# A two-layer graph kernel: the prologue in another order, inverse roots by GpSimd's power

## What is computed

```python
h = relu(layernorm(x))
w_norm = (weight - mean(weight)) / std(weight, ddof=1)
weight_q = quantise to 3 bits and a sign, range wgt_alpha
xq = quantise h to 4 bits, range act_alpha
support = relu(matmul(xq, weight_q))            # scaled by the deltas
support_q = quantise support to 4 bits, range act_alpha2
x1 = x + matmul(adj, support_q)                 # scaled back
out = x1 + attention_layer(relu(layernorm(x1)), adj, ...)
```

## Time and profile before

| | |
|---|---|
| three runs | 160.69, 160.95, 161.58 us; median 160.95 |
| profiled execution | 160.78 us, span 158.9 us |
| mean granted TensorE clock | 0.983 |
| busy, share of the span | TensorE 89%, VectorE 71%, ScalarE 69%, GpSimd 24% |
| DMA | 27.44 MB, mean 173 GB/s |

### The profile page before, as it was taken

The page is one execution under the profiler, slowest core; times in us unless marked ns, Lnnn a source line. Parts: engine busy times, 40 slices in busy tenths (PEclk is TensorE's granted clock), DMA queues, the critical chain, the costliest instruction groups (busy, mean ns, idle before and its releaser), DMA issues.

```text
span 158.9 us, 2206 instructions
## 1 busy us (share of the span) xinstructions
PE 141.7 (89%) x702; PEld 111.9 (70%) x702; DVE 112.1 (71%) x242; ACT 109.2 (69%) x157; POOL 37.4 (24%) x123
## 2 busy tenths in 40 slices
PE   0093999999999999999999999999999999999930
PEld 0093766667676667788888888888888888889920
DVE  0799799898936355997975667876779779624461
ACT  3637878889988587918937999999995966121000
POOL 2134251423320000006070111012016265221100
PEclk9999699999999999999999999999999999999997
DMA  2999999993221100052399899993101101110102
GB/s 47 373 412 416 398 394 426 414 323 55 51 59 40 37 0 0 0 171 97 45 341 400 250 379 359 342 388 144 66 0 66 66 4 66 66 66 0 68 8 68
DMA packets 11982, 27.44 MB, mean 173 GB/s; under 512 B 5184, under 2 KB 5440, under 8 KB 9920
## 3 DMA queue, kind: packets, MB, share of 16 engines
q1 hardware_dynamic: 11824, 27.27, 48.2%
q10 hardware_dynamic: 144, 0.00, 0.0%
HBM read 22.02 MB, written 4.19 MB: 165 GB/s over the span
## 4 chain that ended last, share of the span: by engine, by line
PE 87%; DVE 7%; DMA 3%; issue 1%; SPq 0%; DVEq 0%
PE acc L925 28%; PE acc L927 28%; PE acc L907 9%; PE acc L893 9%; PE acc L908 9%; DMA w_sb<-weight 3%; PE acc L935 2%; PE acc L879 1%; DVE w_st L747 1%; DVE st L679 1%; DVE h_i L704 1%; DVE w_i L750 1%; DVE w_q L756 1%; DVE ring L742 1%; PE acc L938 0%
## 5 line engine op out<-in xcount | busy, mean ns | idle before, releaser
L925 PE MATMUL acc<-sup,hi 128*128 128x512 f32 (+1 forms) x208 | 76.4, 374 | 0.1
L927 PE MATMUL acc<-sup,lo 128*128 128x512 f32 (+1 forms) x208 | 76.3, 373 | 0.0
L925 PEld LDWEIGHTS acc<-sup,hi 128*128 128x128 f32 x208 | 39.2, 188 | 7.3 <-issue 0.5
L927 PEld LDWEIGHTS acc<-sup,lo 128*128 128x128 f32 x208 | 39.2, 188 | 6.8
L370 ACT ACTIVATE junk<-raw,below 128x2048 uint8<-128x2048 f32 x16 | 31.8, 1989 | 0.0
L512 POOL TENSOR_SCALAR nm<-mv 128x1 f32<-128x1 f32 (+2 forms) x20 | 13.3, 665 | 65.8 <-DVE ve L689 65.8
L907 PE MATMUL acc<-sup,hi 128*128 128x512 f32 x64 | 27.9, 436 | 0.0
L720 DVE TENSOR_TENSOR lo<-raw,hi 128x2048 fp32r<-128x2048 f32 x11 | 25.1, 2285 | 2.9 <-ACT hi L359 2.9
L908 PE MATMUL acc<-sup,lo 128*128 128x512 f32 x64 | 25.1, 393 | 0.0
L727 DVE SCALAR_TENSOR_TENSOR ring<-ring,rs,x_sb 128x512 f32<-128x512 f32 x15 | 11.0, 750 | 14.8 <-POOL rs L521 12.2
L359 ACT ACTIVATE hi<-raw 128x2048 fp32r<-128x2048 f32 x11 | 21.0, 1910 | 0.3 <-PE acc L908 0.2
(11 more groups left out here) (78 smaller groups left out, 117.6 us busy)
## 6 DMA issues: line engine op xcount, KB each, us to landing
raw<-adj_t SPq DMA_DIRECT2D x16, 1024.0 KB, 7.0
out<-ring SPq DMA_DIRECT2D x15, 256.0 KB, 4.2
x_sb<-x SPq DMA_DIRECT2D x3, 1024.0 KB, 14.4
w_sb<-weight SPq DMA_DIRECT2D x4, 256.0 KB, 5.0
x_sb<-x SPq DMA_DIRECT2D x2, 256.0 KB, 5.0
x_sb<-x SPq DMA_DIRECT2D x1, 512.0 KB, 6.3
out<-ring SPq DMA_DIRECT2D x2, 128.0 KB, 2.2
h_iT<-h_i SPq DMA_TRANSPOSE x8, 2.4
```

The source lines that it names most:

```text
L925: nc.tensor.matmul(bank[:, cols], part(hi, k % PARTS, j), sup[:, j, cols], start=(j == 0), stop=False)
L927: ins = nc.tensor.matmul(bank[:, cols], part(lo, k % PARTS, j), sup[:, j, cols], start=False, stop=(j == T - 1))
```

## The change

- **Transfers.** The scalars have no transfer of their own; each row of the weight is followed by the four scalars (516 columns instead of 512), and VectorE reads them from block 0. x tile 0 is loaded from ScalarE's queue. SP starts with the weight.
- **Inverse roots.** Reciprocal, Sqrt and refining are replaced by one GpSimd `tensor_tensor` with `ALU.pow` and an exponent of -0.5, in both layers, for the weight and for tile 15. ScalarE's relu takes the quantising constant as its scale, and GpSimd multiplies the negated mean by it.
- **Statistics.** ScalarE sums tiles 0 and 1 (two passes each). VectorE takes two tiles per turn up to j = 5.
- **Order.** TensorE: transposes 0, 24 warm-ups, transposes 1, 6 warm-ups, support 0, support 1, aggregate 0, transposes 2 and 3, aggregate 1, support 2, then for each j support(j-1), transposes(j), aggregate(j-2). Around the sums stand 16 and 12 warm-ups. ScalarE and VectorE are ordered to match.

The diff's core (the renaming of semaphores and tiles is left out):

```diff
-    WARM_SUMS, WARM_FIRST, WARM_T, WARM_S = 14, 14, (12, 4), (0, 12)
+    WARM_SUMS, WARM_FIRST, WARM_T = 16, 12, (24, 6)
...
+        w_sb = sb("w_sb", [P, KD, D + 4], F32)
...
-            load_x(0)
             for k in range(KD):
                 load_w(k)
...
-            def root(n, a, m):
-                act.wait_ge(inverse_ready, n)
-                nc.scalar.activation(rs[:, a:a + m], rv[:, a:a + m], ACT.Sqrt).then_inc(root_ready, 1)
...
+            act.dma_start(x_sb[:, 0, :], x[0:P, :]).then_inc(x_in[0], 16)
+            sums(0)
             relu1(0)
+            sums(1)
             relu1(1)
+            copy_T(0)
             act.wait_ge(w_bias, 1)
             round_w(2)
+            round_w(3)
+            copy_T(1)
+            split_piece(0)
+            relu_sup(0)
+            relu_sup(1)
+            relu1(2)
+            split_piece(1)
+            relu1(3)
+            copy_T(2)
+            copy_T(3)
+            split_piece(2)
+            relu1(4)
+            relu1(5)
+            relu_sup(2)
+            split_piece(3)
+            for j in range(4, T + 2):
+                if j <= T:
+                    relu_sup(j - 1)
                 if j < T:
                     copy_T(j)
...
+            def inverse_root(a, m):
+                nc.gpsimd.tensor_tensor(rs[:, a:a + m], ve[:, a:a + m], minus_half[:, 0:m], ALU.pow).then_inc(r_ready, 1)
...
+            mean_of_sum(0)
+            var_of_squares(0)
+            inverse_root(0, 1)
+            mean_of_sum(1)
+            pool.wait_ge(w_var, 1)
+            nc.gpsimd.tensor_tensor(ws(W_ROOT), ws(W_VAR), minus_half[:, 0:1], ALU.pow).then_inc(w_root, 1)
+            var_of_squares(1)
+            inverse_root(1, 1)
...
-            constants()
             w_stats(0)
+            first_constants()
             chain(w_stats(1))
...
-            wait_x(1)
-            stats_at = step(stats(1))
+            constants()
             dve.wait_ge(w_tot, 2)
...
+            quantise_h(0)
+            dve.wait_ge(w_root, 1)
...
+            chain(nc.vector.tensor_scalar(ws(W_SCALE), ws(W_ROOT), cc(C_W), ((W - 1.0) / W)**0.5, ALU.mult, ALU.mult))
             nc.vector.scalar_tensor_tensor(ws(W_BIAS), ws(W_SCALE), -1.0, ws(W_MEAN), ALU.mult, ALU.mult).then_inc(w_bias, 1)
             rounded = [round_w(k) for k in range(KD // 2)]
+            quantise_h(1)
             for k in range(KD // 2):
                 dve.wait_ge(dve_chain, rounded[k])
                 clip_w(k)
             wait_x(2)
             stats(2)
...
+            normalise(3, stats(3))
+            lo_of_piece(0)
+            quantise_sup(0)
+            wait_x(4)
+            stats(4)
+            lo_of_piece(1)
+            quantise_sup(1)
+            quantise_h(2)
+            quantise_h(3)
+            normalise(4, stats(5))
+            nxt = 6
+            for j in range(3, T + 2):
...
-                for _ in range(2 if 2 <= j < 4 else 1):
+                for _ in range(2 if j <= 5 else 1):
...
+            for j in range(EARLY):
+                transposes(j)
+                warm_up(WARM_T[j])
+            support(0)
+            support(1)
+            aggregate_first(0)
+            transposes(2)
+            transposes(3)
+            aggregate_first(1)
+            support(2)
+            for j in range(4, T + 2):
+                if j <= T:
+                    support(j - 1)
                 if j < TURN:
                     transposes(j)
+                aggregate_first(j - 2)
...
+        "weight": np.concatenate([np.asarray(L0_gnn_weight), np.tile(scalars, (D, 1))], axis=1),
```

More of the change, by code:

```diff
@@ L26, with gnn_kernel @@
 C_RSC, C_RWA, C_RAA, C_RAA2, C_QIN, C_SUP0, C_SUP, C_OUT0, C_OUT, C_W = range(10)
-W_MEAN, W_D, W_SQ, W_VAR, W_INV, W_ROOT, W_SCALE, W_BIAS = range(8)
-def gnn_kernel(nc, x, adj, adj_t, weight, scalars, pairs, wq_t, bq, wk_t, bk, is_pair, out):
+W_MEAN, W_D, W_SQ, W_ND, W_VAR, W_ROOT, W_SCALE, W_BIAS = range(8)
+def gnn_kernel(nc, x, adj, adj_t, weight, pairs, wq_t, bq, wk_t, bk, is_pair, out):
     N, D = x.shape
@@ L377, in relu1 @@
                     act.wait_ge(hq_ready, j - RING + 1)
-                nc.scalar.activation(ring[:, j % RING, :], x_sb[:, j, :], ACT.Relu,
-                                     bias=nm[:, j:j + 1]).then_inc(relu_ready, 1)
+                nc.scalar.activation(ring[:, j % RING, :], x_sb[:, j, :], ACT.Relu, bias=nm[:, j:j + 1],
+                                     scale=cn[:, C_QIN:C_QIN + 1]).then_inc(relu_ready, 1)
             def copy_T(j):
@@ L416, in _, with sums @@
-            act.wait_ge(nm_ready, 1)
-            nc.scalar.activation(junk[:, 0:D], x_sb[:, 0, :], ACT.Square, bias=nm[:, 0:1],
-                                 accum_out=x0s[:, 1:2]).then_inc(x0_squared, 1)
-            relu1(0)
[L420 to L424, removed]
+            def sums(t):
+                act.wait_ge(x_in[t], 16)
+                if t:
+                    act.wait_ge(x_squared, t)
+                nc.scalar.activation(junk[:, 0:D], x_sb[:, t, :], ACT.Copy, accum_out=xs[:, t, 0:1]).then_inc(x_summed, 1)
+                act.wait_ge(x_mean, t + 1)
+                nc.scalar.activation(junk[:, 0:D], x_sb[:, t, :], ACT.Square, bias=xm[:, t:t + 1],
+                                     accum_out=xs[:, t, 1:2]).then_inc(x_squared, 1)
@@ L689, in variance, with normalise @@
                 nc.vector.tensor_scalar(ve[:, a:a + m], mv[:, a:a + m, 1], EPS, None, ALU.add).then_inc(var_ready, 1)
[L691 to L694 removed]
+            def normalise(n, last):
+                variance(mean_var(step(last), *first_ln[n - 1]), *first_ln[n - 1])
             def quantise_h(j):
@@ L803, in _ @@
                 clip_w(k)
-            variance(mean_var(after, *first_ln[2]), *first_ln[2])
-            inverse(3, *first_ln[2])
-            nxt = 4
-            for j in range(T + 2):
+            normalise(3, stats(3))
[10 more added lines that the diff above has]
+            for j in range(3, T + 2):
                 for t in (j + 1, j + 2):
@@ L1019 @@
     adj_t = np.ascontiguousarray(np.concatenate([first, blocks[GT:].reshape(T - GT, P, T * P)]))
+    scalars = np.stack([np.asarray(v) for v in (L0_gnn_adj_scaling_factor, L0_gnn_wgt_alpha, L0_gnn_act_alpha,
+                                                L0_gnn_act_alpha2)])
     arrays = {
```

162 lines of the change are left out of this document (53 added, 109 removed).

## The result

The changed kernel takes 158.53 us (median of four runs, 158.03 to 159.85); the kernel before, on the same chip, 161.24 (four runs, 160.69 to 161.58). The ratio is 0.984, with a 95% interval of 0.980 to 0.988: faster, by 2.7 us. The profiled execution took 158.69 us with a span of 156.9, against 160.78 and 158.9. The forecast was 158.6, within 157.0 to 160.6.

A forecast was written before the change was run, and what follows sets the result against it. TensorE was taken to bound the kernel, leaving only prologue and tail to gain. From 160.78 us: -3.0 (earlier support 0), +1.3 (waits less warm-ups and clock), -0.45 (tail), so -2.2: 158.6 us, range 157.0 to 160.6.

The forecast's parts named there:

- Part 1: Prologue transfers: weight lands at about 4.9 instead of 5.84 us, 1.0 us gained, between 0 and 1.7.
- Part 2: Weight's chain, variance to bias: 0.9 instead of 1.54 us with a 0.25 us power; constants cost 0.2 to 0.3 back.
- The sign of being right: Among the prediction's listed signs, for the inverse roots: a GpSimd power of 0.2 to 0.5 us.
- Part 3: TensorE before support 0: it starts at 13.7 us (12.9 to 14.3), 3.0 us earlier than 16.69.
- The bounds 10.3 and 13.7 us for the rise: TensorE's warm-ups: clock rise between these times puts support 0's start at 12.9 to 14.3 us.
- Part 4: Support 0 to the second stage: TensorE waits 3.6 us in all, stretch 48.8 us, 1.3 more than before.
- Part 5: Tail behind the last matmul: power replaces reciprocal, root and refinements; 0.45 us saved, 0.4 if held, 0.6 if not.
- transfers not earlier: Rival, prologue: slow first 2.5 us belong to any start; support 0 at 14.5 to 15.0, 159.4 to 160.1 us; chance 0.17.
- the clock falls again: Rival, new waits behind support 0: clock fall costs 1.7 us, giving 160.3 us, no change; chance 0.10.
- The slow power: Rival, GpSimd's power: at 2 us long the kernel takes 162.7 us; decides from about 1.4 us on; chance 0.13.

The follow-up runs named there:

- the two with a stand of 0.79 us on the way: Changed kernel with the scalars' broadcast put back behind x tile 0, 159.99 us; changed kernel with h_i of tile 0 behind the bias, 161.36 us.
- the kernel with 2.73 us: Changed kernel with ScalarE's copy of piece 1 ahead of relu of tile 2: 157.59 us, ratio 0.978 to the kernel before.

## Why the prediction was right

The forecast of 158.6 us was right to 0.1, by the median and by the profiled execution (158.69), and the chosen mechanism (an earlier weight, a shorter chain to the bias, three new waits behind support 0, a shorter tail) is the one the traces show. The gain was less exact: 2.2 us were forecast, 2.1 lie between the two profiled executions and 2.7 between the medians, since the four runs of the kernel before have a median of 161.24 and not 160.95. That the median came so close is luck to that extent, and several terms were off and cancelled.

- **Part 1, transfers:** 1.0 us was taken of at most 1.7. The first statistic came 1.6 us earlier (4.28 for 5.86), but the fourth, which ends this part of the chain, waits for its data until 7.03 us and came 0.98 us earlier. So the chain got the 1.0 us that was taken, while the first block got nearly all of the 1.7.
- **Part 2, the weight's chain:** the power was mis-sized, 0.55 to 0.58 us when nothing runs beside it and 0.82 here, where 0.25 was taken (bounds 0.20 and 1.94). The sign of being right, a power of 0.2 to 0.5 us, failed. From the variance's end to the bias's end 1.34 us pass instead of 0.9; before, it was 1.74 (the sum's 1.54 began at the reciprocal's end), so 0.4 us were saved and not 0.6. The power is held by h_i of tile 0: moved away, 0.58 and 1.10 us. The bias ended at 10.97, forecast 10.9, because another error went the other way: the 0.2 to 0.3 us for the two constants were not paid, since VectorE had to wait for block 3 anyway.
- **Part 3, support 0:** forecast 13.7, range 12.9 to 14.3, measured about 12.9. The warm-ups took 1.50 us, the early end: at the low rate they are 2.77, in two other runs. The bounds 10.3 and 13.7 us for the rise stand on no row: the earlier trace rows show warm-ups at the low rate until 13.49 us and a transpose at the full rate only at 16.23. With the same prologue the 24 warm-ups took from 1.50 to 2.73 us, so that support 0 came at the early end was luck. Support 0 isn't the gate that the prediction made of it, however. In the kernel with x tile 0 on SyncE's queue the warm-ups took 2.25 us and support 0 started at 13.37, 0.5 us later than in the change, and the second stage still started 51.38 us behind the bias's last operation, against 51.42 in the change, 51.39 with the power doubled and 51.39 with the centring moved. What sets the second stage is the chain of the other engines' work from the bias on, VectorE's above all with ScalarE and GpSimd between, as long as the supports don't fall behind it.
- **Part 4, behind support 0:** forecast waits 0.5, 1.3, 1.5 and 0.15 twice; measured 0.74, 0.77 and 1.25, and none beyond. The stretch took 49.3 us instead of 48.8. The places were right and the sum was 2.8 instead of 3.6 us; the work between them was counted 1.1 us short (45.2; the windows from 12.85 to 62.2 us hold 46.3 us of busy TensorE). The first two supports have 0.3 of it (2.06 us busy for 1.76); for the rest I found no single cause. Between the first and second wait stands a term that the walk left out, the pair's negated mean on GpSimd: 0.88 us beside lo, and 0.27 where nothing runs beside it, as in the kernel with h_i of tile 0 behind the bias.
- **Part 5, the tail:** 0.45 forecast, 0.25 measured at the start of the last result, in the change and with the powers alone, and nothing at the end of the span. It is the power again: the sum had the result about 0.2 us behind the centring's end, and it came 0.43 behind it (152.44 for 152.01). The rule of the Trainium skill, GPSIMD Engine Reference, section Specifications, that I weighed speaks of two-input or two-port VectorE operations. The trace agrees: beside the two-input lo the negated mean took 0.88 us instead of 0.27, and the power beside the centring 0.72 instead of 0.55. Not every VectorE operation does it: tile 0's power, with a statistic beside it, took 0.57 us. That the centring runs in a two-port mode no row says; it takes 0.48 us for 512 columns, a statistic 0.69.
- **The rivals:** "transfers not earlier" fell with the first statistic at 4.28 us, "the clock falls again" with 1.00 in every window from 8 us to the last matmul. The slow power fell with its size; the first power of the kernel (tile 0's, at 6.81 us) took 0.57 us, so the Trainium skill's 6 us for a first call (same page, section Instruction dispatch) doesn't show here.

That the clock stays up in the change was forecast, for the reason that work lies between the waits, and the kernel with the old turns fits that: one stand of 2.43 us, and a fall. When the rate first rises is another matter, and not settled. The 24 warm-ups took 1.50, 1.50, 1.65, 1.71, 1.91, 2.12, 2.25 and 2.73 us in eight kernels whose prologue up to there is the same but for a few tenths, with no stand of TensorE on the way; in the two with a stand of 0.79 us on the way they took 2.77. So a stand goes with a late rise, but a late rise comes without one too. Nor does a late rise alone cost much: in the kernel with 2.73 us the second stage still starts 51.16 us behind the bias. Whether the changed kernel's own scatter of 1.8 us comes from this wasn't tried.

## What to carry to other kernels

Where engines take turns, find the chain of work that the waiting engine hangs on, and measure from the event that starts it: here the time from the bias to the second stage was the same to 0.04 us in four kernels, though in one of them support 0 came 0.4 us later behind the bias. An operation that leaves the queue of a full engine is worth its own time even where its substitute on an idle engine is slower. Data that lands earlier is worth only what the last block of it gains, less the work that had been hidden in the wait. A fixed number of filler matmuls is a bet on the clock: the same 24 took 1.50 us, or 2.77 and stood in the way of real work.

## What the runs showed of the hardware

GpSimd's power on one column takes 0.54 to 0.58 us, also beside a VectorE statistic; it takes 0.72 to 0.82 where a one-input VectorE operation from f32 (h_i or the centring, 512 columns) runs beside its first part, but 0.58 beside a rounding of the weight that starts together with it. On two columns it takes 0.70 to 0.72, also beside a statistic, mostly 0.87 to 1.00 beside h_i, and 1.17 once beside the two-input lo; on four 1.01 to 1.04. With the 144 small packets of a broadcast to 128 partitions among them, the transfers move 256 instead of 342 GB/s between 4.50 and 7.50 us. TensorE's matmuls leave their low rate at different moments in nearly the same program, and the profile's granted clock doesn't tell: it reads 1.00 between 8 and 12 us in the kernel without warm-ups too, while a transpose of a tile there takes 0.63 us against 0.40 later.
